# Moving 25 of 35 tile transposes of a gated cross-attention and MLP kernel from TensorE to DRAM and VectorE

## The chip, the cores and the metric

The kernel runs on one core of one Trainium2 chip. The metric is the time of one launch on the device in microseconds (us); lower is better.

## The reference

2048 tokens of 512 features pass through two residual layers, all in float32.

```python
# layer 1: one of 4 experts per token, picked by token id; Wg = Wu = Wd = ctx_2048[e]  (512 x 512)
h = layernorm(x)
z = h @ ctx[e].T
x = x + tanh(g_xattn) * ((silu(z) * z) @ ctx[e].T)
# layer 2: a gated MLP, 512 -> 1408 -> 512
h = layernorm(x)
g = (h @ gate_w.T) * gate_s
u = (h @ up_w.T) * up_s
x = x + tanh(g_ffn) * (((silu(g) * u) @ down_w.T) * down_s)
```

## The kernel before

**Routing.** Up to about 12 us the kernel counts the tokens of each expert and builds index tables. The tokens are laid out so that each tile of 128 belongs to one expert: at most 19 tiles (`STEPS`). `gidx` tells which row of x is in each place, `sidx` where it goes.

**Precision.** A float32 value is split in a high word (ScalarE, a copy to fp32r) and a low word (VectorE, the difference). An expert product has three passes (high by high, low by high, high by low) of four matmuls, `expert_product`, L970. In the MLP the weights have no low words with these inputs, so each product has two passes.

**Expert phase, 12 to 142 us.** In step k TensorE runs `first_product(k)`, the turn of tile k+1's normed rows (`turn_x`, L961, four 128x128 transposes through PSUM, matmuls at L967), `second_product(k-1)`, and `turn_h(k)` (four transposes, L996). VectorE's `step(k)` (L747) is, in order: low word of h of k-1 (L736), norm of k+1 (L684), wait for the gathered rows of k+2, their statistics (L673 and two small ones), `hidden(k)` (L732, wanted by `turn_h(k)`), low word of x of k+1 (L710), and `update(k-1)` (L743), which waits for the second product. ScalarE makes the high words and the silu, and beside them rounds and checks the MLP weights. GpSimd, in a loop of two rounds of six steps (L389), computes 1/std (L362), gathers the rows of tile k+4 (L351) once tile k-2 is stored, and stores tile k-1 (L356) after its update. It copies the two index columns into `inow` at each step (L396, L398). The rows live in a ring of six slots.

**MLP phase, 142 to 389 us.** There are four blocks of four tiles, and each block has 11 chunks of 128 inner features. In chunk c TensorE runs 8 gate and 8 up matmuls (L1077), then the 8 down matmuls of chunk c-1 (L1084). In the first three blocks the tiles of the next block are prepared beside the chunks (`PREP_AT`): statistics and norm at chunks 5 to 8 after the chunk's own VectorE work, `turn_x` on TensorE after the gate and up matmuls of chunks 6 to 9, then high and low words. In block 0 VectorE also makes the low words of the weights (L828). Block 0's own four tiles are turned at the end of the expert phase (L957).

**SyncE's queue** issues plain DMAs in a fixed order, each behind its waits: the expert weights, small inputs, then weight rows (704 KB each) and rows of the down weights to be checked (256 KB each), the rows of the next block, the down weights.

**Counts.** There are 19 + 16 = 35 turns of x, 4 of them by `first_turn_x`, and 19 turns of h.

## Time and profile before

| what | value |
|---|---|
| median of 3 runs | 399.51 us (399.36 to 400.72) |
| the profiled execution | 398.89 us, its span 397.1 us |
| TensorE busy (matmuls, weight loads) | 374.2 us (94%), 305.9 us (77%) |
| VectorE busy | 232.2 us (58%) |
| ScalarE, GpSimd busy | 144.4 us (36%), 84.8 us (21%) |
| mean granted TensorE clock | 0.995 |
| turns of x by L967, 124 matmuls | 19.4 us busy |

Times are of one execution. Busy is the share of the span in which an engine ran an instruction; an engine that has little idle time and ends most waits sets the time.

### The profile page before, as it was taken

What the parts mean: (1) busy time and instruction counts of PE and PEld (TensorE: products, weight loads), DVE (VectorE), ACT (ScalarE), POOL (GpSimd) and SP (SyncE); (2) the same over time, 40 slices, a digit from 0 to 9 for tenths busy, and PEclk for the clock granted to TensorE, in tenths of its full rate; (3) what the DMA queues carried; (4) which work ended last, traced back from release to release, by engine and by line L of the source; (5) the groups of instructions that cost most, each with busy time, mean ns of one, the idle gap of its engine ahead of it and who ended that gap; (6) DMA issues with size and microseconds to landing.
All of it is one profiled execution on the core that took longest, in us unless ns stands there. A gap on an engine that the chain in (4) does not pass through costs nothing.

```text
span 397.1 us, 5787 instructions
## 1 busy us (share of the span) xinstructions
PE 374.2 (94%) x1771; PEld 305.9 (77%) x1771; DVE 232.2 (58%) x441; ACT 144.4 (36%) x263; POOL 84.8 (21%) x130
## 2 busy tenths in 40 slices
PE   3479899999999999999999999999999999999993
PEld 2357688888888878877788888888888888888882
DVE  6878857567877578867647235636225635422225
ACT  4455556565545244522322223322323222222220
POOL 6333544444452120000102101101201001200003
PEclk9999999999999999999999999999999999999998
DMA  6759767461221126210001210000120000100002
GB/s 212 258 188 295 239 210 277 143 213 61 102 79 54 54 83 221 79 68 0 2 1 53 104 55 0 1 0 26 79 106 0 0 0 0 80 26 0 0 0 109
DMA packets 13807, 34.56 MB, mean 87 GB/s; under 512 B 2272, under 2 KB 2272, under 8 KB 13792
## 3 DMA queue, kind: packets, MB, share of 16 engines
q1 hardware_dynamic: 9472, 20.21, 14.9%
q0 software_dynamic: 4320, 14.16, 9.7%
q8 instruction: 8, 0.13, 0.1%
q14 instruction: 7, 0.06, 0.0%
HBM read 25.19 MB, written 9.18 MB: 87 GB/s over the span
## 4 chain that ended last, share of the span: by engine, by line
PE 86%; DVE 6%; DMA 4%; issue 2%; SPq 1%; POOL 1%; ACT 0%; DVEq 0%; POOLq 0%; ACTq 0%
PE bank L1077 39%; PE bank L981 23%; PE bank L1084 19%; PE bank L967 3%; DMA dsb<-down_s 3%; PE bank L996 2%; DVE work L760 1%; DMA rows<-x,gidx 1%; DVE wgu L828 1%; DVE sh L841 1%; PE bank L957 0%; DVE xn L684 0%; DMA ids_i<-ids 0%; DVE rows L875 0%; DVE tmp L868 0%
## 5 line engine op out<-in xcount | busy, mean ns | idle before, releaser
L1077 PE MATMUL bank<-work,wgu 128*128 (+1 forms) x720 | 167.2, 385 | 0.1
L1077 PEld LDWEIGHTS bank<-work,wgu 128*128 128x128 f32 x720 | 133.0, 188 | 27.9 <-issue 0.5
L981 PE MATMUL bank<-work,parts 128*128 (+1 forms) x432 | 111.0, 406 | 2.3 <-DVE work L760 1.5
L981 PEld LDWEIGHTS bank<-work,parts 128*128 128x128 f32 x432 | 79.7, 191 | 19.9 <-issue 2.9
L1084 PE MATMUL bank<-work,hp 128*128 128x512 f32 x352 | 88.5, 394 | 0.5 <-DVE hp L846 0.5
L841 DVE SCALAR_TENSOR_TENSOR sh<-bank,gs,sh 128x512 f32<-128x512 f32 (+1 forms) x45 | 33.2, 738 | 78.8 <-PE bank L1077 78.8
L1084 PEld LDWEIGHTS bank<-work,hp 128*128 128x128 f32 x352 | 65.1, 188 | 13.9 <-DVE hp L846 0.9
L543 ACT ACTIVATE sh<-bank,gs 128x512 f32<-128x512 f32 (+1 forms) x45 | 30.5, 677 | 84.8 <-PE bank L1077 84.0
L547 ACT ACTIVATE hp<-sh 128x512 fp32r<-128x512 f32 (+1 forms) x45 | 28.0, 622 | 88.3 <-DVE sh L841 88.3
L846 DVE TENSOR_TENSOR hp<-sh,hp 128x512 fp32r<-128x512 f32 (+1 forms) x45 | 30.6, 680 | 30.2 <-ACT hp L547 30.0
L362 POOL TENSOR_TENSOR rstd<-ve,half 128x1 f32<-128x1 f32 x31 | 18.6, 599 | 126.7 <-DVE ve L678 126.1
L433 POOL DMA_INDIRECT out<-rows,oidx x16 | 16.1, 1008 | 116.2 <-DVE rows L875 93.6
L743 DVE SCALAR_TENSOR_TENSOR rows<-bank,tg,rows 128x512 f32<-128x512 f32 (+1 forms) x19 | 14.2, 749 | 21.4 <-PE bank L981 21.4
L463 ACT ACTIVATE parts<-bank 128x512 fp32r<-128x512 f32 x19 | 11.4, 599 | 33.0 <-PE bank L996 31.1
L967 PE MATMUL bank<-ident,xn 128*128 128x128 f32 x124 | 19.4, 280 | 3.6 <-DVE xn L684 3.5
L967 PEld LDWEIGHTS bank<-ident,xn 128*128 128x128 f32 x124 | 15.1, 142 | 9.4 <-DVE xn L684 4.8
L684 DVE TENSOR_SCALAR xn<-rows,mv,rstd 128x512 f32<-128x512 f32 (+1 forms) x31 | 16.9, 547 | 9.0 <-POOL rstd L362 9.0
L673 DVE BATCH_NORM_STATS2 bn<-rows 128x6 f32<-128x512 f32 (+1 forms) x31 | 21.2, 685 | 1.5 <-DMA rows<-x,gidx 1.5
L467 ACT ACTIVATE sh<-bank 128x512 f32<-128x512 f32 x19 | 11.4, 598 | 16.6 <-PE bank L981 11.9
L732 DVE TENSOR_TENSOR sh<-bank,sh 128x512 f32<-128x512 f32 x19 | 13.1, 688 | 5.0 <-ACT sh L467 4.6
L356 POOL DMA_INDIRECT x_rows<-rows,inow x12 | 12.3, 1028 | 11.8 <-DVE rows L743 10.0
L351 POOL DMA_INDIRECT rows<-x,inow x12 | 12.5, 1040 | 10.0 <-POOL inow L398 9.2
(126 smaller groups left out, 251.9 us busy)
## 6 DMA issues: line engine op xcount, KB each, us to landing
wraw<-guT SPq DMA_DIRECT2D x8, 704.0 KB
ctx_in<-ctxT SPq DMA_DIRECT2D x4, 1024.0 KB, 5.4
rows<-x_rows SPq DMA_DIRECT2D x8, 512.0 KB, 3.5
checked<-dwT SPq DMA_DIRECT2D x11, 256.0 KB
rows<-dwT SPq DMA_DIRECT2D x11, 256.0 KB, 2.6
dsb<-down_s SPq DMA_DIRECT2D x1, 256.0 KB
out<-rows,oidx POOLq DMA_INDIRECT x16, 2.7
rows<-x,inow POOLq DMA_INDIRECT x12
```

The source lines that it names most:

```text
L362: pool.tensor_tensor(rstd[:, 0:1], ve[:, 0:1], half[:, :], ALU.pow)\
L433: pool.indirect_dma_start(out, bass.IndirectOffsetOnAxis(ap=oidx[:, BLOCK * b + t:BLOCK * b + t + 1], axis=0), rows[:, row_slot(b, t), :], ...
L543: act.activation(sh[:, part], gate_ps(i)[:, part], ACT.Silu, scale=gs[:, 0, c:c + 1])\
L547: act.activation(hslot(c)[:, 0, part], sh[:, part], ACT.Copy)\
L673: dve.bn_stats(bn[:, 0, :], rows[:, ds(at, 1), :]).then_inc(S["bn_parts"], 1)
L684: dve.tensor_scalar(xn[:, :], rows[:, ds(at, 1), :], mv[:, 0, 0:1], rstd[:, 0:1], ALU.subtract, ALU.mult).then_inc(S["xn_ready"], 1)
L841: dve.scalar_tensor_tensor(out=sh[:, part], in0=up_ps(i)[:, part], scalar=gs[:, 1, c:c + 1], in1=sh[:, part], op0=ALU.mult, op1=ALU.mult). ...
L846: dve.tensor_tensor(hslot(c)[:, 1, part], sh[:, part], hslot(c)[:, 0, part].bitcast(F32), ALU.subtract)\
L967: mm = pe.transpose(xt_ps[:, c * P:(c + 1) * P], xn[:, c * P:(c + 1) * P], ident[:, :])
L981: mm = pe.matmul(out_ps[:, :], part(s)[:, c * P:(c + 1) * P], ctx_w(e, c, w), start=n == 0, stop=n == last)
L1077: mm = pe.matmul(out_ps[:, tiles.start * P:tiles.stop * P], wgu[:, row + h, w, c * P:(c + 1) * P], moving, start=n == 0, stop=n == last)
L1084: mm = pe.matmul(acc_ps[u][:, :], hslot(c)[:, s, u * P:(u + 1) * P], down_w(c, w), start=c == 0 and n == 0, stop=c == IC - 1 and n == len( ...
```

## The change

The turns of tiles 6 to 18 and of the 12 tiles of blocks 1 to 3 (25 in all) leave TensorE. The normed rows `xn` (128x512) are written by SyncE to a DRAM scratch in four column quarters (512 runs of 512 B), and read back so that partition 32i+a holds quarter i of rows 4a to 4a+3 (128 runs of 2 KB). One VectorE instruction then transposes all 32x32 blocks. Both sides of it are read and written at a stride of 16 B. In the result, partition p of part c holds feature 4p+c, and so the weights are loaded in that order, and the transposes that stay on TensorE read every fourth column.

VectorE norms a step earlier (k+2) and takes the statistics of k+3 in step k. GpSimd's loop is unrolled, reads the index tables directly, and gathers 16 rows once near its beginning. SyncE's list of loads is interleaved with the write and the read of each tile.

```diff
+TURN_AT = {c + 2: t for c, t in PREP_AT.items()}
+ON_PE = 6
-    ctx_v = ctxT.rearrange("e (c p) f -> e p c f", p=P)
-    gu_v = guT.rearrange("(r p) n -> p r n", p=P)
+    turned = nc.dram_tensor("turned_rows", [TURNED, QUADS, P, P], F32).ap()
+    ctx_v = ctxT.rearrange("e (p c) f -> e p c f", c=KC)
+    gu_v = guT.rearrange("(s p h) n -> s h p n", s=2, h=KC)
+        def every_fourth(a, c):
+            return a[:, :].rearrange("p (q c) -> p c q", c=KC)[:, c, :]
@@ SyncE
-            sp.wait_ge(S["ctx_lo"], EXPERTS * KC)
-            for r in range(5, 2 * KC):
-                check_row(r)
-                weight_row(r)
-            check_row(8)
+            def turn_rows(m):
+                n = m - ON_PE
+                sp.wait_ge(S["xn_ready"], m + 1)
+                sp.dma_start(turned[n].rearrange("i p c -> p i c"),
+                             xn[:, :].rearrange("p (i c) -> p i c", i=QUADS)).then_inc(S["xn_out"], 16)
+                sp.wait_ge(S["xn_out"], 16 * (n + 1))
+                if n:
+                    sp.wait_ge(S["xt_ready"], n)
+                sp.dma_start(quarter_home(m < STEPS),
+                             turned[n].rearrange("i (a g) c -> (i a) (g c)", g=QUADS)).then_inc(S["xq_in"], 16)
-            sp.wait_ge(S["stored"], 16 * (BLOCK + EXPERTS - 1))
-            load_rows(0)
-            for c in range(9, IC):
-                check_row(c)
+            for m in range(ON_PE, STEPS):
+                turn_rows(m)
+                if m - 1 < IC:
+                    check_row(m - 1)
+                if m == 9:
+                    sp.wait_ge(S["ctx_lo"], EXPERTS * KC)
+                if m in (9, 11, 13):
+                    weight_row((m + 1) // 2)
+                if m == 10:
+                    sp.wait_ge(S["stored"], 16 * (BLOCK + EXPERTS - 1))
+                    load_rows(0)
             ...
+                for t in range(BLOCK):
+                    turn_rows(STEPS + BLOCK * (b - 1) + t)
@@ GpSimd
+            pool.memset(inow[:, :], 0).then_inc(S["early_index"], 1)
+            pool.wait_ge(S["early_index"], 1)
+            pool.indirect_dma_start(
+                rows[0:16, ring_slot(5), :], None, x,
+                bass.IndirectOffsetOnAxis(ap=inow[0:16, :], axis=0)).then_inc(S["early_row"], 16)
-            with pool.Fori(0, 2) as i:
-                ...
+            for k in range(2, STEPS + 1):
+                if k < ON_PE:
                     inverse_std(k + 2)
                 if k == NORM_AT:
                     first_inverse_std()
+                pool.wait_ge(S["stored"], 16 * (k - 1))
                 if k + 4 < STEPS:
                     pool.wait_ge(S["x_landed"], 16 * (k + 4 - FIRST))
                     gather(ring_slot(k + 4), gidx[:, k + 4:k + 5])
+                if ON_PE - 1 <= k < STEPS - 3:
+                    inverse_std(k + 3)
                 pool.wait_ge(S["rows_ready"], k)
                 store(ring_slot(k - 1), sidx[:, k - 1:k])
@@ ScalarE
+            def turned_hi(m, home, part):
+                act.wait_ge(S["xt_ready"], m - (ON_PE - 1))
+                act.activation(part, home, ACT.Copy).then_inc(S["xhi_ready"], 1)
@@ VectorE
+            def turn(m, expert):
+                dve.wait_ge(S["xq_in"], 16 * (m - (ON_PE - 1)))
+                dve.wait_ge(S["xlo_ready"], m)
+                dve.transpose(turned_home(expert).rearrange("p (h a g) -> p g h a", h=KC, g=QUADS),
+                              quarter_home(expert).rearrange("p (g b h) -> p g h b", g=QUADS, h=KC))\
+                   .then_inc(S["xt_ready"], 1)
+            def step(k):
+                h_lo(k - 1)
+                norm(k + 2, ring_slot(k + 2))         # waits for xn_out of the tile before
+                landed(k + 3)
+                stats(k + 3, ring_slot(k + 3))
+                turn(k + 1, True)
+                hidden(k)
+                turned_lo(k + 1, True, tile_x(1), tile_x(0))
                 update(k - 1)
             ...
+                    if not last:                      # MLP, ahead of chunk(b, c)
+                        if c in TURN_AT:
+                            next_turn(b + 1, TURN_AT[c])
+                        if c in PREP_AT:
+                            next_stats(b + 1, PREP_AT[c])
+                        if c in TURN_AT:
+                            next_x_lo(b + 1, TURN_AT[c])
+                        if c in PREP_AT:
+                            next_norm(b + 1, PREP_AT[c])
                     chunk(b, c)
@@ TensorE
-                mm = pe.transpose(xt_ps[:, c * P:(c + 1) * P], xn[:, c * P:(c + 1) * P], ident[:, :])
+                mm = pe.transpose(xt_ps[:, c * P:(c + 1) * P], every_fourth(xn, c), ident[:, :])
-                turn_x(k + 1)
+                if turns:
+                    turn_x(k + 1)
-                        if c - 1 in PREP_AT:
-                            with pe.If(b < BLOCKS - 1):
-                                turn_x(STEPS + BLOCK * b + PREP_AT[c - 1])
```

## Rows read from the trace of the kernel before

**Rows 1.** The page: busy shares, and the chain that ended last by engine.
```profile
PE 374.2 (94%) x1771; PEld 305.9 (77%) x1771; DVE 232.2 (58%) x441; ACT 144.4 (36%) x263; POOL 84.8 (21%) x130
PE 86%; DVE 6%; DMA 4%; issue 2%; SPq 1%; POOL 1%; ACT 0%; DVEq 0%; POOLq 0%; ACTq 0%
```

**Rows 2.** Chain in order of time, expert steps: start us, us, what.
```profile
62.66 0.44 PE bank L967 x4
63.10 2.78 PE bank L981 x12
...
69.09 0.44 PE bank L967 x4
```

**Rows 3.** The same chain in block 1 of the MLP.
```profile
229.98 1.81 PE bank L1084 x8
...
235.42 1.81 PE bank L1084 x8
...
240.86 0.44 PE bank L967 x4
241.30 1.85 PE bank L1084 x8
```

**Rows 4.** Timeline of TensorE, block 0: start us, us, engine, line, tiles.
```profile
171.85 1.98 PE L1084 MATMUL bank<-work,hp 128*128 128x512 f32 x8
...
197.03 2.11 PE L1084 MATMUL bank<-work,hp 128*128 128x512 f32 x8
```

**Rows 5.** Timeline of VectorE in an expert step; in brackets idle before.
```profile
59.66 0.75 DVE L743 SCALAR_TENSOR_TENSOR rows<-bank,tg,rows 128x512 f32 x1 [1.47 <-PE bank L981]
...
61.16 0.54 DVE L684 TENSOR_SCALAR xn<-rows,mv,rstd 128x512 f32 x1
...
61.62 0.68 DVE L673 BATCH_NORM_STATS2 bn<-rows 128x6 f32 x1
...
62.66 0.15 DVE L678 TENSOR_SCALAR ve<-mv 128x1 f32<-128x1 f32 x1
...
63.33 0.69 DVE L732 TENSOR_TENSOR sh<-bank,sh 128x512 f32<-128x512 f32 x1 [0.51 <-ACT sh L467]
```

**Rows 6.** GpSimd's DMAs, expert steps: timeline, then landing times of L351, L356.
```profile
61.24 1.00 POOL L356 DMA_INDIRECT x_rows<-rows,inow  x1 [1.08 <-DVE rows L743]
...
65.45 1.03 POOL L351 DMA_INDIRECT rows<-x,inow  x1 [0.83 <-POOL inow L398]
...
77.98 1.04 POOL L351 DMA_INDIRECT rows<-x,inow  x1 [0.85 <-POOL inow L398]
...
83.45 0.18 POOL L396 COPY inow<-gidx 128x1 uint32 x1 [0.70 <-DMA rows<-x,inow]
...
DMA to landing us min/median/max: 3.6/3.9/4.1
...
DMA to landing us min/median/max: 2.7/2.8/4.6
```

**Rows 7.** The page's DMA issues: count, KB each, median us to landing.
```profile
rows<-x_rows SPq DMA_DIRECT2D x8, 512.0 KB, 3.5
...
rows<-dwT SPq DMA_DIRECT2D x11, 256.0 KB, 2.6
```

**Rows 8.** Timeline of VectorE, two chunks of block 0 in a row.
```profile
184.10 0.75 DVE L841 SCALAR_TENSOR_TENSOR sh<-bank,gs,sh 128x512 f32<-128x512 f32 x1 [0.17 <-PE bank L1077]
...
190.29 0.75 DVE L841 SCALAR_TENSOR_TENSOR sh<-bank,gs,sh 128x512 f32<-128x512 f32 x1
```

**Rows 9.** Weight loads of TensorE: a strided f16 operand, a dense f32 one.
```profile
6.55 1.17 PEld L943 LDWEIGHTS bank<-token,is_low 128*128 128x128 f16 x16 [3.08 <-DVE is_low L617]
...
62.27 0.59 PEld L967 LDWEIGHTS bank<-ident,xn 128*128 128x128 f32 x4
```

**Rows 10.** Timeline of the beginning: the second gather, the gates.
```profile
10.58 1.67 POOL L351 DMA_INDIRECT rows<-x,gidx  x1 [0.47 <-DVE gidx L649]
...
26.14 0.20 ACT L506 ACTIVATE tg<-gg 128x2 f32<-128x2 f32 x1 [0.80 <-DMA dsb<-down_s]
```

More of the change, by code:

```diff
@@ L52 @@
 PREP_AT = {5: 0, 6: 1, 7: 2, 8: 3}
+TURN_AT = {c + 2: t for c, t in PREP_AT.items()}
+ON_PE = 6
+TURNED = STEPS - ON_PE + TILES - BLOCK
+QUADS = 4
 def ring_slot(k):
@@ L219, in tile_h, with quarter_home, turned_home @@
             return parts[:, 2 + s, :]
+        def every_fourth(a, c):
+            return a[:, :].rearrange("p (q c) -> p c q", c=KC)[:, c, :]
+        def quarter_home(expert):
+            return xq0[:, :] if expert else rows[:, RING - 2, :]
+        def turned_home(expert):
+            return xt0[:, :] if expert else rows[:, RING - 1, :]
         def ctx_w(e, c, s):
@@ L512, in step @@
                 silu(k)
-                x_hi(k + 1)
-            with act.Fori(1, IC + 1) as k:
+                if on_pe:
+                    x_hi(k + 1)
+                else:
+                    turned_hi(k + 1, turned_home(True), tile_x(0))
+            with act.Fori(1, ON_PE - 1) as k:
+                step(k, on_pe=True)
+                down_check(k - 1)
+            with act.Fori(ON_PE - 1, IC + 1) as k:
                 step(k)
@@ L551, in mlp_block @@
                 for c in range(IC):
+                    if c in TURN_AT and not last:
+                        t = TURN_AT[c]
+                        turned_hi(STEPS + BLOCK * b + t, turned_home(False), xpart(b + 1, (t + 2) % BLOCK, 0))
                     chunk(b, c)
@@ L555, in mlp_block @@
                             down_hi(d)
-                    if c - 1 in PREP_AT and not last:
-                        t = PREP_AT[c - 1]
-                        next_x_hi(STEPS + BLOCK * b + t, b + 1, (t + 2) % BLOCK)
             mlp_block(0, first=True)
@@ L753, in step @@
                 x_lo(k + 1)
+                if k == ON_PE - 2:
+                    norm(k + 2, ring_slot(k + 2))
+                update(k - 1)
+                if k == ON_PE - 2:
+                    landed(k + 3)
+                    stats(k + 3, ring_slot(k + 3))
+            def step(k):
+                looped = not isinstance(k, int)
+                h_lo(k - 1)
+                if looped or k + 2 < STEPS:
+                    norm(k + 2, ring_slot(k + 2))
+                if looped or k + 3 < STEPS:
+                    landed(k + 3)
+                    stats(k + 3, ring_slot(k + 3))
+                turn(k + 1, True)
+                hidden(k)
+                turned_lo(k + 1, True, tile_x(1), tile_x(0))
                 update(k - 1)
@@ L781, in _ @@
             dve.wait_ge(S["gates_ready"], 1)
-            step(1)
+            step_on_pe(1)
             ctx_lo(9, 12)
-            step(2)
+            step_on_pe(2)
             ctx_lo(12, 16)
@@ L787, in _ @@
             dve.tensor_copy(oidx[:, :], bank[4][:, 0:TILES]).then_inc(S["oidx_ready"], 1)
-            with dve.Fori(3, STATS_AT) as k:
+            step_on_pe(3)
+            step_on_pe(4)
+            with dve.Fori(ON_PE - 1, STATS_AT) as k:
                 step(k)
@@ L804, in _ @@
             h_lo(16)
-            norm(18, ring_slot(18))
+            turn(18, True)
             dve.wait_ge(S["loose_step"], 1)
@@ L1034, in _ @@
             for k in range(1, EXPERTS):
-                expert_step(k, *experts_at(k), ctx_ready=KC * (k + 1))
-            with pe.Fori(EXPERTS, 15) as k:
+                expert_step(k, *experts_at(k), ctx_ready=KC * (k + 1), turns=True)
+            expert_step(EXPERTS, *experts_at(EXPERTS), turns=True)
+            with pe.Fori(EXPERTS + 1, 15) as k:
                 expert_step(k, *experts_at(k))
```

93 lines of the change are left out of this document (36 added, 57 removed).

## The prediction

> **What bounds the kernel now.** I read the busy shares first, then the chain that ended last. TensorE is busy 94% of the span and carries 86% of the chain [rows 1]; VectorE, at 58%, has room. So each microsecond taken from TensorE's queue between 28 and 389 us comes back, as long as nothing that feeds TensorE becomes later. I then read the chain in order of time, where the pace is very regular. An expert step is turn 0.44, product 2.78, turn of h 0.44, product 2.78: from the turn at 62.66 to the next at 69.09 are 6.43 us [rows 2]. In the MLP a chunk without a turn takes 5.44 us (229.98 to 235.42), one with a turn in blocks 1 and 2 takes 5.88 (235.42 to 241.30) [rows 3]. In block 0 the timeline shows more: four chunks with turns last from 171.85 to 197.03, 25.18 us, or 6.3 each [rows 4]. There VectorE sets the pace, for its own cycle is 6.19 us, from 184.10 to 190.29, and the turn waits for the norm at its end [rows 8].
>
> **The turns that leave.** Expert phase: 13 turns (tiles 6 to 18) x 0.44 = 5.7 us. Blocks 1 and 2: 8 x (5.88 - 5.44) = 3.5 us. Block 0: 25.18 - 4 x 5.44 = 3.4 us, if VectorE's work there is no longer awaited within the chunk. Gross gain 12.6 us. An expert step would then take 6.43 - 0.44 = 5.99 us.
>
> **The new way of a tile.** Norm, write to DRAM, read back, VectorE transpose. The trace has none of the last three.
> - The write is 256 KB in 512 B runs. Nearest rows: a 256 KB load with 2.6 us [rows 7] and the row stores with 2.7 to 4.6, median 2.8 [rows 6]. I take 2.8.
> - The read is 256 KB in 2 KB runs: 2.6 (512 KB take 3.5 [rows 7], the upper bound).
> - The transpose has 128x512 elements on both sides. By VectorE's passes of that shape it lasts 0.54 to 0.75 [rows 5]; I take 0.69, as a two-input pass, with double (1.4) as the upper end and 0.54 as the lower.
>
> With 0.54 for the norm and 0.1 for each of SyncE's two issues the trip lasts 0.54 + 0.1 + 2.8 + 0.1 + 2.6 = 6.1 us. Norm starts at 61.16 and the statistics after it end at 62.81 [rows 5], so the transpose stands 1.65 us behind the norm's place, one step on: 5.99 + 1.65 = 7.6 us are there. Slack 1.5 us. SyncE is held in its queue during the trip, with a check row, weight row or block rows behind it; each of those is wanted two or more steps later, so I cost this at nothing. The other way round, a weight row of 704 KB or block rows (512 KB, 3.5 us [rows 7]) can lie ahead of the next write, in four steps; the slack covers about 1.5 us of that.
>
> **VectorE in an expert step.** It gains the transpose and loses nothing. Before, it stood idle 1.47 ahead of the update and 0.51 ahead of `hidden` [rows 5], together 1.98 of 6.43; now 5.99 - (6.43 - 1.98) - 0.69 = 0.85 idle is left. It still fits, but `hidden(k)`, which `turn_h(k)` waits for, now stands behind the transpose and behind the wait for the gathered rows of tile k+3, one tile further ahead than before. This is the tightest place of the change. The chain, from the end of a second product: update 0.21 + 0.75 (the product ended at 62.66 - 2.78 - 0.44 = 59.44, the update at 59.66 + 0.75 = 60.41 [rows 2, 5]), store's issue 0.83 later at 61.24, landing 2.8, gather's start 0.83, landing 3.6, statistics 1.19 (61.62 to 62.81), transpose 0.69, hidden 0.69: 11.6 us [rows 5, 6]. Two steps are 12.0. So the slack is 0.4 us. Before, the chain had a whole step more. Not every gather lands in 3.6: the one at 77.98 was waited for until 83.45, 5.5 us, as block rows were loading [rows 6], and DRAM traffic now grows by 512 KB per step. Some gathers will be late by about 1 us. There are 11 such steps; I take a quarter late by 0.9: 2.5 us lost. The ends are 0 and 11 x 0.8 = 8.5 (next part).
>
> **The crossing.** Tile 6 is the first to take the trip. Its norm stands behind the low word of x in step 4. In step 6 that ends near 64.6 (0.6 behind `hidden`, 63.33 + 0.69), two steps of 6.43 earlier at 51.7. So the transpose can start at 51.7 + 6.1 = 57.8 and `hidden(5)` ends at 59.2. `turn_h(6)` started at 65.88 (63.10 + 2.78); `turn_h(5)`, a step and a turn earlier, wants its input at 59.0 [rows 2, 5]. With the handovers 0.5 us is lost once (0 to 2.5, with a 4.6 us write).
>
> **Strided reads.** 19 turns of h and 10 of x stay on TensorE and now load every fourth f32, a stride of 16 B. The nearest row: 16 loads of 128 f16 columns at a stride of 32 B last 1.17 us, 73 ns each [rows 9], below the 110 ns (0.44/4) at which dense transposes follow each other [rows 2]. So I expect nearly nothing: 29 x 0.035 = 1.0 us. The upper end is a doubled turn, 29 x 0.44 = 12.8. A gain has no source here: lower end 0.
> On this stride the Trainium skill speaks against the change: "Advanced Engine Details and Errata", SBUF Cachelines, has 16-byte lines of which each needs two hits in a row for full rate, and here each gets one. The strided row at 73 ns leaves that open, since its elements are half as wide. If the rule holds fully for the f32 loads, it is the second rival below.
>
> **Block 0's VectorE.** The transpose adds 0.69 to 6.19, but the low word of x now stands between statistics and norm and fills the wait for GpSimd's 1/std; I take 6.4 us for chunks 7 and 8, 5.7 for 5 and 6, 5.2 for 9. Against 5.44 it falls behind by at most 2.5 us. TensorE first notices when the product behind down 1.81 and gate 1.81 waits for `h`, 0.75 long: 3.62 - 0.75 = 2.9 us. So it is hidden; 0.3 for the near miss, 1.5 if the transpose takes 1.4.
>
> **Beginning.** The extra gather can shorten the second one's issue (1.67 against the usual 1.03 [rows 6, 10]), but 1/std of tile 0 waits for statistics anyway: 0, at the ends -0.7 and +0.7. The copies to `inow` that go free GpSimd 0.36 us per step; counted in the chain above. Expert weights in 8 KB runs may land earlier and with them the scales that ScalarE waited 0.80 for [rows 10]: gain 0.3 (0 to 0.8).
>
> **The sum.** 12.6 - 2.5 - 0.5 - 1.0 - 0.3 + 0.3 = 8.6. The profiled execution took 398.89, so 390.3; the median of the runs is 0.6 above it: **390.9 us**.
>
> **Rivals.**
> 1. *The gather chain sets every step.* If landings are 5.5 us throughout, the chain is 13.5, a step 6.75 in 11 steps: 11 x (6.75 - 5.99) = 8.4 lost in place of 2.5: 396.8. For it: the slack of 0.4 and more traffic. Against: most landings at 3.6 to 4.1 [rows 6], and fewer loads after step 12.
> 2. *Strided f32 reads run at half rate.* 12.8 in place of 1.0: 402.7, slower than before. Against it: the 73 ns.
> 3. *The trip is too long* (the other side as well). It decides from 6.43 + 1.65 = 8.1 us on: then `hidden` waits in each expert step for the read. With a write of 4.6 [rows 6] and a read of 3.5 [rows 7] plus 0.7 for the norm and issues, 8.8, a step is 7.15, 13 x (7.15 - 5.99) = 15.1 lost in place of 2.5 for gathers: 403.5. MLP chunks have two chunks, 10.9 us, for the trip, so no loss there. Against it: both medians.
>
> **Chances.** Forecast 0.66, first rival 0.15, second 0.08, third 0.08, something else 0.03. About 0.5% (2.0 us) can be told from no change, so faster means below 397.5: 0.66 and most of the first rival, 0.76. Same 0.11, slower 0.13. The lower end of the range is the gain without losses, 12.6 + 0.8 = 13.4: 386. The upper, 400, takes in the first rival and a mild form of the others.
>
> **What would show it.** Right: expert steps of 6.0 us in the chain, with no wait of TensorE's transposes of h for `hidden`; L967's count down from 124 to 24 matmuls; chunks of 5.44 in all blocks. Wrong: the transpose far over 0.7; TensorE waiting for `hidden`, and VectorE ahead of it for gathered rows (first rival) or for the read (third); transposes of more than 0.44 per four (second). The prediction falls if an expert step is above 6.3 us, or the transpose above 1.4.

## The result, and the profile after

The changed kernel takes 403.67 us (401.01 to 406.84, 11 runs) where the kernel before takes 399.30 (398.06 to 400.72, 11 runs): ratio 1.0112, 95% interval 1.0077 to 1.0147. 390.9 was predicted, the range ended at 400. It is slower by 1.1%, though TensorE has 100 fewer matmuls to do. The medians and ratios below leave out executions that took over 1.5% more than the fastest of the same kernel (one of `before_traffic`, two of `copy_turn`, one of `all_dense_late`).

The profiled execution took 403.7 us, its span is 402.0 (before 397.1), its mean granted clock 0.984 (before 0.995). The page of the changed kernel, busy shares and chain by engine, answers to [rows 1]:

```profile
PE 370.5 (92%) x1671; PEld 301.8 (75%) x1671; DVE 257.8 (64%) x466; ACT 146.4 (36%) x263; POOL 84.0 (21%) x108
PE 63%; DVE 15%; DMA 13%; issue 4%; ACT 2%; POOL 2%; DVEq 0%; SPq 0%; POOLq 0%
```

TensorE's busy time fell by only 3.7 us for 100 matmuls less, and its share of the chain from 86% to 63%. DMAs now hold 13%. The chain says where: it runs through stores and gathers of the expert phase (7% and 3%).

**Where the time went.** Three marks in both traces divide the span: the turn of h of tile 4 (52.86 before, 52.39 after), the first gate matmul of the MLP (142.53 and 152.04) and the end (397.1 and 402.0). The beginning gained 0.5 us. The expert steps between the first two marks went from 89.67 to 99.65 us: 10.0 lost. The MLP went from 254.6 to 250.0: 4.6 gained. The sum is the 4.9 us of the spans. So one half of the change does nearly what it should, and the other loses more than that.

Timeline of TensorE in the changed kernel's expert phase (start us, us, engine, line, tiles; in brackets the idle time before and what ended it). It answers to [rows 2]. L1064 is the turn of h, L1049 the products:

```profile
60.09 0.75 PE L1064 MATMUL bank<-ident,sh 128*128 128x128 f32 x4 [1.57 <-DVE sh L773]
61.01 7.37 PE L1049 MATMUL bank<-work,parts 128*128 x24 [0.17 <-issue]
...
90.22 0.74 PE L1064 MATMUL bank<-ident,sh 128*128 128x128 f32 x4 [3.43 <-DVE sh L773]
91.10 7.34 PE L1049 MATMUL bank<-work,parts 128*128 x24
99.38 0.75 PE L1064 MATMUL bank<-ident,sh 128*128 128x128 f32 x4 [0.94 <-DVE sh L773]
100.30 5.70 PE L1049 MATMUL bank<-work,parts 128*128 x24 [0.17 <-issue]
...
107.87 0.75 PE L1064 MATMUL bank<-ident,sh 128*128 128x128 f32 x4 [1.87 <-DVE sh L773]
108.75 7.38 PE L1049 MATMUL bank<-work,parts 128*128 x24
...
122.62 5.73 PE L1049 MATMUL bank<-work,parts 128*128 x24
...
128.57 5.75 PE L1049 MATMUL bank<-work,parts 128*128 x24
```

The last two rows are a step of the size that was predicted: 128.57 - 122.62 = 5.95 us. Earlier TensorE waits for `hidden` (L773), four times between 60 and 108: 1.57, 3.43, 0.94 and 1.87, together 7.8 us. And behind each of the three longer waits the next 24 matmuls last 7.4 us in place of 5.7: another 4.9 us. The turn of h behind a wait is slower too: 0.9 us from its start to the product's (60.09 to 61.01) in place of 0.39 (128.18 to 128.57); once, at 80.17, it is so without a wait. Windows of the same trace show what the slow products are (busy us of PE, PEld, DVE, ACT, POOL, then the granted clock, the DMA share, GB/s):

```profile
75.00:100.00 25.00, 20.32 (x84) 15.73 (x82) 15.31 (x27) 11.62 (x24) 6.31 (x8) 0.93 0.79 246
...
125.00:150.00 25.00, 25.00 (x126) 20.93 (x125) 21.64 (x40) 12.35 (x23) 6.86 (x8) 1.00 0.40 127
```

Windows of 1 us show it plainly: the granted clock is 1.00 up to 61 us, 0.62 from 61 to 62, 0.50 from 62 to 64, 0.67 from 64 to 65 and 1.00 from 65 on; behind the other two long waits it is 0.50 from 92 to 95, and 0.51 and 0.50 from 109 to 112. So after these idle times the engine was granted its lower level (1.2 of 2.4 GHz) for some 3 us of the next product. The expert steps of before have no such wait and no such product. The wait's price is thus not its length: 1.57 us of waiting cost 1.57 + 0.5 for the turn + 1.6 for the product.

The eight steps from 52.78 to 116.36 take 63.6 us, 15.8 more than eight of 5.97; less the 5.7 that 13 turns gained, that is the 10.0 lost. Of the 15.8, 7.8 are waits, 4.9 slow products and 2.6 slow turns (five of 0.5).

**What `hidden` waits for.** GpSimd's timeline: L391 stores, L386 gathers, L397 is 1/std.

```profile
82.66 0.96 POOL L386 DMA_INDIRECT rows<-x,gidx  x1 [6.02 <-DMA x_rows<-rows,sidx]
83.65 0.58 POOL L397 TENSOR_TENSOR rstd<-ve,half 128x1 f32<-128x1 f32 x1
84.41 1.05 POOL L391 DMA_INDIRECT x_rows<-rows,sidx  x1 [0.18 <-issue]
91.93 0.97 POOL L386 DMA_INDIRECT rows<-x,gidx  x1 [6.47 <-DMA x_rows<-rows,sidx]
...
93.68 1.04 POOL L391 DMA_INDIRECT x_rows<-rows,sidx  x1 [0.18 <-issue]
```

From store to store are 93.68 - 84.41 = 9.3 us, and ahead of the stores GpSimd waits for nothing (0.18, "issue"): it isn't VectorE's updates that are late but GpSimd's own loop, and of its 9.3 us 7.3 are the landing of the store, without which the next gather may not start (the gather overwrites the slot). The other parts of the loop (gather's issue, 1/std, handovers) take 2.0. The chain that ended last passes through this loop three times before it comes back to `hidden`:

```profile
75.60 6.81 DMA x_rows<-rows,sidx
...
82.66 0.96 POOL rows L386
...
84.41 7.26 DMA x_rows<-rows,sidx
...
93.68 7.72 DMA x_rows<-rows,sidx
...
101.66 3.31 DMA rows<-x,gidx
...
106.13 1.13 DVE xt L756
...
107.27 0.56 DVE sh L773
```

Landing times of the stores (L391) in the changed kernel, to be read beside the last of [rows 6]:

```profile
DMA to landing us min/median/max: 2.7/3.4/7.7
```

The medians of the stores (2.8 and 3.4) hide it; the long ones, 6.8, 7.3 and 7.7 us, follow each other. (The 4.6 of [rows 6] is the very first store, at 36.1 us; from 60 to 130 us the stores of before take 2.7 to 3.4.) The gathers are less late: those issued at 82.66 and 91.93 are there when VectorE's statistics, which wait for them, start at 87.35 and 96.48, so 4.7 and 4.6 us. The landing row of the gathers in [rows 6] (3.6/3.9/4.1) holds only the two at 9.0 and 10.6 us, ahead of the expert steps. The first of TensorE's four waits, at 60.09, is another: its chain goes through the write of the first trip, 3.87 us from 51.74, and then norm, statistics and transpose. SyncE's queue shows what goes beside them (L316 read of the trip, L292 check row, L323 block rows, L285 weight row, L311 write of the trip):

```profile
83.16 0.33 SPq L316 DMA_DIRECT2D xq<-turned_rows  x1
83.57 0.38 SPq L292 DMA_DIRECT2D checked<-dwT  x1
84.01 0.95 SPq L323 DMA_DIRECT2D rows<-x_rows  x2
85.11 0.55 SPq L311 DMA_DIRECT2D turned_rows<-xn  x1
92.44 0.33 SPq L316 DMA_DIRECT2D xq<-turned_rows  x1
92.87 0.38 SPq L292 DMA_DIRECT2D checked<-dwT  x1
93.30 0.43 SPq L285 DMA_DIRECT2D wraw<-guT  x1
94.17 0.38 SPq L311 DMA_DIRECT2D turned_rows<-xn  x1
```

SyncE is held by the trip: from 85.11 to 92.44 it waits for the write of the trip to land (7.3 us, where 2.8 was assumed; an undisturbed one at 119.0 took 2.2), and then four to five transfers go out within 2 us, at 84 and at 93, just as GpSimd issues its store. From 75 to 100 us the DMA engines are busy for 0.79 of the time, from 125 to 150 for 0.40. That the trips' bytes make the stores late is so far a reading of one trace; experiment 3 tests it.

**VectorE's transposes**, groups of the changed kernel (xcount | busy us, mean ns | idle before):

```profile
L756 DVE STREAM_TRANSPOSE xt<-xq 128x512 f32<-128x512 f32 x13 | 14.7, 1128 | 1.0 <-DMA xq<-turned_rows 0.9
L756 DVE STREAM_TRANSPOSE rows<-rows 128x512 f32<-128x512 f32 x12 | 13.3, 1105 | 0.0
```

1.13 and 1.11 us, not 0.69. **The MLP**: the chain in block 1 answers to [rows 3], and VectorE's in block 0 to [rows 8]:

Block 1, start us, us, what:

```profile
229.67 3.63 PE bank L1146 x16
233.30 1.81 PE bank L1153 x8
235.11 3.63 PE bank L1146 x16
```

Block 0:

```profile
187.69 0.76 DVE sh L902
...
194.55 0.76 DVE sh L902
...
201.41 0.76 DVE sh L902
```

Chunks of 5.44 in blocks 1 and 2, as predicted; but 6.86 us for VectorE's cycle in chunks 7 and 8 of block 0, where 6.4 was expected and 6.19 was before.

### The profile page after: what moved, and what is told of

It is laid out like the page before. It is cut to its first block, busy times and chain, and to the rows that moved or that the text cites. A ratio compares the mean times of both kernels' runs of the same rounds, so it can differ in the third digit from the quotient of the medians.

```text
span 402.0 us, 5526 instructions
## 1 busy us (share of the span) xinstructions
PE 370.5 (92%) x1671; PEld 301.8 (75%) x1671; DVE 257.8 (64%) x466; ACT 146.4 (36%) x263; POOL 84.0 (21%) x108
## 4 chain that ended last, share of the span: by engine, by line
PE 63%; DVE 15%; DMA 13%; issue 4%; ACT 2%; POOL 2%; DVEq 0%; SPq 0%; POOLq 0%
PE bank L1146 31%; PE bank L1153 15%; PE bank L1049 15%; DMA x_rows<-rows,sidx 7%; DMA rows<-x,gidx 3%; DVE wgu L889 2%; DMA rows<-dwT 2%; DVE work L819 1%; DVE sh L902 1%; PE bank L1064 1%; DVE bn L705 1%; POOL rstd L397 1%; ACT hp L579 1%; DMA turned_rows<-xn 1%; DVE xt L756 1%
## 5 line engine op out<-in xcount | busy, mean ns | idle before, releaser
L1049 PE MATMUL bank<-work,parts 128*128 (+1 forms) x432 | 111.6, 414 | 2.9 <-DVE work L819 1.4
L1049 PEld LDWEIGHTS bank<-work,parts 128*128 128x128 f32 x432 | 84.1, 199 | 22.7 <-issue 4.2
L1153 PE MATMUL bank<-work,hp 128*128 128x512 f32 x352 | 87.1, 389 | 0.5 <-DVE hp L907 0.5
L397 POOL TENSOR_TENSOR rstd<-ve,half 128x1 f32<-128x1 f32 x31 | 21.1, 679 | 104.8 <-DVE ve L710 102.5
L386 POOL DMA_INDIRECT rows<-x,gidx x19 | 20.0, 1051 | 46.8 <-DMA x_rows<-rows,sidx 38.7
L391 POOL DMA_INDIRECT x_rows<-rows,sidx x19 | 19.4, 1022 | 35.9 <-DVE rows L784 28.7
L1064 PE MATMUL bank<-ident,sh 128*128 128x128 f32 x72 | 12.2, 292 | 9.5 <-DVE sh L773 9.5
L1064 PEld LDWEIGHTS bank<-ident,sh 128*128 128x128 f32 x72 | 10.8, 207 | 12.4 <-DVE sh L773 11.6
L480 ACT ACTIVATE work<-rows 128x512 f32 (+1 forms) x12 | 7.6, 632 | 27.1 <-DVE rows L756 27.1
```

The lines of the kernel that those rows point to most:

```text
L386: pool.indirect_dma_start(rows[:, at, :], None, x, bass.IndirectOffsetOnAxis(ap=index, axis=0))\
L391: pool.indirect_dma_start(scratch, bass.IndirectOffsetOnAxis(ap=index, axis=0), rows[:, at, :], None)\
L397: pool.tensor_tensor(rstd[:, 0:1], ve[:, 0:1], half[:, :], ALU.pow)\
L1049: mm = pe.matmul(out_ps[:, :], part(s)[:, c * P:(c + 1) * P], ctx_w(e, c, w), start=n == 0, stop=n == last)
L1064: mm = pe.transpose(ht_ps[:, c * P:(c + 1) * P], every_fourth(sh, c), ident[:, :])
L1153: mm = pe.matmul(acc_ps[u][:, :], hslot(c)[:, s, u * P:(u + 1) * P], down_w(c, w), start=c == 0 and n == 0, stop=c == IC - 1 and n == len( ...
```

## The experiments

All were timed beside the kernel before, whose median is given with each (398.8 to 399.3). Theory stands for the explanation of the moment; it changed on the way.

**1. The two halves apart.** `mlp_only` is the kernel before with the 12 MLP turns moved and the new feature order; experts and GpSimd as before.

```diff
+ON_PE = STEPS                       # tiles 0 to 18 stay on TensorE
```


> Only the 12 turns of the MLP phase go by DRAM and VectorE; the expert phase, GpSimd's loop and SyncE's early order are those of the kernel before (the strided reads of the turns left on TensorE stay). Theory (the loss of the whole change lies in the expert phase, +10.0 us there, and the MLP phase gained 4.6): about 4 us faster than before, near 395.5, with chunks of 5.44 us in blocks 1 and 2. Rival (the DRAM trips or the longer VectorE queue cost in the MLP phase too, or the strided reads cost): no gain, 398 to 401.

Measured 395.94 against 398.92, ratio 0.9909 (0.9877 to 0.9941), as the theory had it. So the MLP half gains 3.0 us net, and the expert half loses 403.7 - 395.9 = 7.8 by itself.

**2. Traffic, and late statistics.** `small_trip` is the changed kernel, with the trips cut to 8 columns of a row; `stats_late` puts the wait for the gathered rows behind `hidden`.

```diff
 # small_trip
-  sp.dma_start(turned[n].rearrange(...), xn[:, :]...)
+  sp.dma_start(turned[n, 0][:, 0:8], xn[:, 0:8])
 # stats_late: step(k)
-  landed(k + 3); stats(k + 3, ...)
   turn(k + 1, True)
   hidden(k)
+  landed(k + 3); stats(k + 3, ...)
```


> The kernel after, with every write and read of the trip cut to 8 columns (4 KB in place of 256 KB) and the transpose reading a constant tile, so the output is not the reference's. All waits, the order of the queues and the 1.13 us transposes stay. Theory (the 512 KB per step, in one burst with a weight row, a check row and GpSimd's store, hold the store up to 7.7 us and so set GpSimd's loop at 9.3 us): stores land in about 3 us again, the expert phase from turn_h(4) to the first gate matmul falls from 99.7 to about 88 us, total 391 to 393. Rival (the longer VectorE chain or the later weight rows make the steps long, not the traffic): at most 3 us gained, total over 399.

> The kernel after, with the wait for gathered rows and the statistics of tile k+3 moved behind hidden(k). Theory (GpSimd's own loop of store, landing, gather, 1/std sets the period in steps 8 to 11): steps there stay near 9 us, the total moves by less than 2 us from 403.7. Rival (hidden(k) standing behind the gather wait sets the steps): the wait of turn_h for hidden, 9.5 us, goes, total 394 to 397.

Measured 398.88 against 398.92 (0.9985, 0.9954 to 1.0016): the bytes of the trips are worth 4.8 us. The theory had 391 to 393 and missed by 6: without the trips' bytes the three stores from 77 to 93 us still land in 4.5, 6.1 and 6.3 us, beside the held loads. `stats_late`: 399.66 (1.0006, 0.9975 to 1.0036): 4.0 us, where the theory gave under 2. It had taken GpSimd's loop for the sole bound; but a part of its lateness is passed on only since `hidden` stands behind the wait for rows that it doesn't need. And with that wait gone another shows. VectorE waited 0.9 us in all for the reads of the trips in the changed kernel, in `stats_late`:

```profile
DVE xt L756 <- DMA xq<-turned_rows: 8.6, 7, 2.7
```

(us in total, times, longest.) Its longest chain to `hidden` is a trip: a write of 7.65 us from 86.07 and a read of 4.19 behind it. The trip's own lateness stood hidden behind the store's.

**3. The same traffic in the kernel before.** `before_traffic` makes all of the expert trips (nothing uses them) with SyncE's order of the changed kernel; the turns stay on TensorE. `before_hold` is the same with trips of 8 columns.

```diff
+  for m in range(6, STEPS):
+      trip(m)                       # write xn, wait, read back; 8 columns in before_hold
+      if m - 1 < IC: check_row(m - 1)
+      ...                           # weight rows at 9, 11, 13, block rows at 10
```


> The kernel before, with the trip's write and read of 256 KB each added for tiles 6 to 18 at the places of the kernel after in SyncE's queue, their data unused. Norm waits for the write of the tile before. TensorE still turns, and statistics keep their old place. Theory (traffic alone holds up GpSimd's stores, but the old order has a step more of slack in front of the statistics): stores land in 5 us or more in steps 8 to 11, yet GpSimd's loop then sets a few of the steps too, so 3 to 8 us slower than before, 402 to 407. Rival (the loss comes from the new order of VectorE, which the old order does not have): within 1.5 us of before although the stores land late.

> The kernel before with SyncE's queue held as in the kernel after (same waits, same order of check, weight and block rows behind the trip of each tile 6 to 18), but the trip is 8 columns (4 KB) each way. The same with full 256 KB trips took 410.0 us, 11 us over before. Theory (both are needed: the held queue puts the large loads next to GpSimd's store, and the 512 KB lengthen the burst): 1 to 4 us over before, stores landing in up to 6 us. Rival (holding alone does it): 8 us or more over before. Other rival (traffic alone): within 0.5 us of before.

Measured 409.51 against 398.92 (1.0218, 1.0159 to 1.0278), above the theory's 402 to 407, and 400.38 against 398.78 (1.0049, 1.0024 to 1.0073). The profiled executions are the longest of `before_traffic` (412.05) and the shortest of `before_hold` (398.47); so their traces show the kind of the difference, the medians its size. Landing times of the stores in `before_traffic`:

```profile
DMA to landing us min/median/max: 2.7/4.5/8.8
```

and in `before_hold`:

```profile
DMA to landing us min/median/max: 2.7/2.8/3.7
```

This is the clearest pair: the same waits, the same order of loads, and 9.1 us between them by the medians (6.7 by the ratios, from three executions). GpSimd's store to store time with traffic, in steps whose own work is unchanged (L372 stores):

```profile
78.32 1.00 POOL L372 DMA_INDIRECT x_rows<-rows,inow  x1 [0.30 <-issue]
...
88.52 1.01 POOL L372 DMA_INDIRECT x_rows<-rows,inow  x1 [0.30 <-issue]
...
99.86 1.00 POOL L372 DMA_INDIRECT x_rows<-rows,inow  x1 [0.31 <-issue]
```

10.2 and 11.3 us where a step is 6.43. So the traffic makes a loss of this kind without VectorE's new order and without the unrolled loop, and the chain of this trace runs through the stores' landings; what the new order adds is the 4.0 us of `stats_late`. The held queue alone costs 1.6 (1.0 to 2.9 by the interval). Whether the changed kernel would lose less with GpSimd's old loop wasn't tried.

**4. Spreading the burst.** `weights_early` issues the last three weight rows in steps 6, 7 and 8 (from 9, 11, 13); `two_quarters` gives the trip two landing buffers, so that SyncE's read doesn't wait for the transpose before; `two_quarters_late` adds the late statistics.

```diff
 # weights_early
-  if m in (9, 11, 13): weight_row((m + 1) // 2)
+  if m in (6, 7, 8):   weight_row(m - 1)
 # two_quarters
-  if n: sp.wait_ge(S["xt_ready"], n)
+  free = n - 1 if m < STEPS else n
+  if free > 0: sp.wait_ge(S["xt_ready"], free)
```


> The kernel after, with weight rows 5, 6 and 7 issued behind tiles 6, 7 and 8 in place of 9, 11 and 13. Theory (bursts that hold a weight row or block rows beside the trip hold up the stores): the late stores move to the steps near 56 to 75 us and the steps after 100 us become 6 to 6.5 us; the total moves by -3 to +1 us. Rival (the trip's own traffic is enough, whatever lies beside it): the stores stay at 7 us in steps 9 to 11, total unchanged within 1 us.

> The kernel after with two buffers for the read quarters in the expert phase, so that SyncE issues the read as soon as the write has landed and no longer waits for the transpose of the tile before; the check, weight and block rows behind it are issued up to 3 us earlier, away from GpSimd's store. VectorE's steps 5 to 9 are unrolled for it. Theory (the large loads collide with the store by the held queue): 2 to 5 us faster than after, 399 to 402. Rival (the number of bytes per step decides, not the moment): within 1 us of after.

> two_quarters, and the statistics of tile k+3 behind hidden(k) as in stats_late, which gave 4 us alone. Theory (the two remedies act on different waits): 395 to 397, as good as the kernel that moves only the MLP's turns. Rival (both remove the same stalls): no better than stats_late, 399 to 401.

Measured: `weights_early` 407.24 against 399.17 (1.0182), 3.6 us worse than the changed kernel, a miss: TensorE waits 10.6 us for `hidden` in its trace, in place of 7.8. That 704 KB more beside a trip cost more than they saved later is the likely reading, not a tested one. `two_quarters` 401.80 against 398.78 (1.0074, 1.0046 to 1.0101), `two_quarters_late` 398.94 (0.9985, 0.9964 to 1.0006), not the 395 to 397 of its theory and no better than `stats_late` by more than the noise. Its stores still take up to 7.3 us to land, but the chain that ended last hardly goes through them any more: from 50 to 145 us it holds 19.6% of writes and 11.7% of reads of the trip and 4.9% of stores, where the changed kernel has 4.1% of writes and 22.9% of stores. Its longest wait for `hidden`, 4.0 us at 95.88, stands behind a write of 7.6 and a read of 4.5 us. With late statistics it is the trip itself that is too long.

**5. The smaller terms.** `copy_turn` puts a dense elementwise pass in the transpose's place. `pool_only` and `stride_only` are the kernel before with GpSimd's part, and with the new feature order and strided reads of TensorE, alone.

```diff
 # copy_turn
-  dve.transpose(turned_home(expert)..., quarter_home(expert)...)
+  dve.tensor_tensor(turned_home(expert), quarter_home(expert), quarter_home(expert), ALU.max)
 # stride_only
-  xn[:, c * P:(c + 1) * P]
+  every_fourth(xn, c)
```


> The kernel after, with the 32x32 transpose replaced by a dense elementwise pass of the same tile (about 0.68 us in place of 1.13), so the output is not the reference's. Theory (GpSimd's loop sets the disturbed steps, VectorE only the chunks of block 0): 1 to 3 us faster than after, 401 to 402.5. Rival (the transpose, 0.44 us over the 0.69 that was reckoned, sets the steps): 13 x 0.44 and more, 6 us or more faster.

> The kernel before with GpSimd's part alone changed: loop unrolled, index tables read directly, one gather of 16 rows near the beginning. Theory (GpSimd is not on the path in the kernel before): within 1 us of before, the beginning up to 0.5 us earlier. Rival (the early gather makes the first gathers cheaper, or the unrolled code costs): 1.5 us or more to either side.

> The kernel before with the new feature order alone: weights and expert weights loaded in that order, all 54 turns on TensorE reading every fourth column. Four transposes went from 0.44 to 0.48 us in the trace of after. Theory: 54 x 0.04 = 2 us slower, 401 to 402, if the extra shows in every turn. Rival (the skill's rule of 16-byte lines holds in full, a turn doubles): 54 x 0.44 = 24 us slower. Other rival: no difference, as the expert weights land earlier in 8 KB runs.

Measured: `copy_turn` 400.75 against 399.17 (1.0047, 1.0013 to 1.0081): the 0.44 us that each transpose takes beyond the assumed 0.69 is worth 2.9 us (2.6 by the ratios). In the traces the first gate matmul comes 1.5 us earlier (150.50 for 152.04) and the MLP takes 1.6 less. `pool_only` 398.67 (0.9994, 0.9981 to 1.0008): nothing. `stride_only` 400.43 (1.0040, 1.0025 to 1.0056): 1.3 us for 54 turns. Its group of TensorE's weight loads, to be read beside the 0.59 us for four of [rows 9]:

```profile
L971 PEld LDWEIGHTS bank<-ident,xn 128*128 128x128 f32 x124 | 19.4, 206 | 7.6 <-DVE xn L688 4.1 <-issue 1.7
```

A strided load takes 206 ns, a dense one 0.59 / 4 = 148 in that row and 142 on average in the same group of the kernel before, but the turn only goes from 0.44 to 0.47 us.

**6. Why the transpose is slow.** `dense_transpose` is `mlp_only` with dense operands of the transpose. The other two keep the reference's feature order: in `mlp_dense_in` the norm writes its columns in quarter order, so that the transpose reads densely; `mlp_dense` also reads the rows back in another order, in four DMAs with runs of 512 B, so that it writes densely too. TensorE reads without a stride in both.

```diff
 # dense_transpose
-  dve.transpose(turned_home().rearrange("p (h a g) -> p g h a", ...), quarter_home().rearrange("p (g b h) -> p g h b", ...))
+  dve.transpose(turned_home(), quarter_home())
 # mlp_dense_in: norm, then the input of the transpose
+  to = to.rearrange("p (i c b) -> p c i b", i=QUADS, c=KC)
+  frm = frm.rearrange("p o (c i b) -> p (o c) i b", i=QUADS, c=KC)
-  quarter_home().rearrange("p (g b h) -> p g h b", ...)
+  quarter_home().rearrange("p (g h b) -> p g h b", ...)
 # mlp_dense: further
+  for i in range(QUADS):
+      sp.dma_start(quarter_home()[32 * i:32 * i + 32, :].rearrange("a (g c) -> a g c", g=QUADS),
+                   turned[n][:, P * i:P * i + P].rearrange("(g a) c -> a g c", g=QUADS))
-  turned_home().rearrange("p (h a g) -> p g h a", ...)
+  turned_home().rearrange("p (h g a) -> p g h a", ...)
```


> mlp_only (396 us) with VectorE's transpose reading and writing dense columns in place of every fourth, so the blocks are laid out wrongly. Theory (the 1.10 us of the transpose are the operation's own): the transpose stays at 1.0 to 1.15 us, the total within 0.5 us. Rival (the 16 B stride on both sides slows it, by the skill's rule of 16-byte lines): 0.6 to 0.7 us, and 1 to 2 us less in total, out of block 0.

> Before's feature order and dense TensorE reads everywhere, the 12 MLP turns moved as in the change; the norm writes its columns in the order quarter, chunk, 32 (runs of 128 B), so that the transpose reads dense rows; it still writes with a stride of 16 B. Theory (each side's stride costs the same): transposes of 0.9 us. Rival 1 (the read's stride costs all 0.40): 0.70. Rival 2 (the write's): 1.10. The strided reads of TensorE that go are worth 1.4 us, so 394 to 395 by either, 395.9 less 1.4 = 394.5.

> As the one before it, and the read of the trip takes rows in another order (four DMAs with runs of 512 B; the write has runs of 2 KB), so that the transpose is dense on both sides. Theory: transpose 0.70 us; chunks 5 to 9 of block 0, where VectorE sets the pace, become 0.40 shorter each, so 1 to 1.6 us beside the 1.4 of the strided reads: 395.9 - 1.4 - 1.3 = 393.2. Rival (runs of 512 B on the read make the trip longer than the two chunks it has): TensorE waits in the chunks, 395 to 397.

Measured: `dense_transpose` 394.31 against 398.78 (0.9871, 0.9842 to 0.9900), its transposes 0.70 us, both as the rival had it; `mlp_dense_in` 394.34 against 399.25 (0.9869, 0.9844 to 0.9894); `mlp_dense` 392.82 against 399.25 (0.9842, 0.9819 to 0.9864). The group of the transposes in `mlp_only`:

```profile
L760 DVE STREAM_TRANSPOSE rows<-rows 128x512 f32<-128x512 f32 x12 | 13.3, 1107 | 0.0
```

in `mlp_dense_in`:

```profile
L760 DVE STREAM_TRANSPOSE rows<-rows 128x512 f32<-128x512 f32 x12 | 12.9, 1079 | 0.0
```

and in `mlp_dense`:

```profile
L761 DVE STREAM_TRANSPOSE rows<-rows 128x512 f32<-128x512 f32 x12 | 8.5, 704 | 0.0
```

The stride of 16 B costs 0.03 us on the read (1.11 to 1.08) and 0.38 on the write: the second rival of `mlp_dense_in`. `mlp_dense` gains 6.4 us on the kernel before, and is the fastest that computes the whole.

**7. What is left of the loss.** `small_late` takes both causes away: trips of 8 columns, two buffers, late statistics. `from_13` is the changed kernel, with the trips of the expert phase begun at tile 13, behind the weight and block rows.

```diff
 # from_13
-ON_PE = 6
+ON_PE = 13
```


> The changed kernel with double quarter buffers, statistics of tile k+3 behind the hidden product, and trips of 8 columns (it leaves out the rest of the trip; the transposes read another buffer): neither the traffic nor the wait of hidden for gathered rows is left. Theory: small trips alone gave 398.9, late statistics alone 399.7, against 403.7; the two causes overlap, since late rows hurt through that wait, so together 395 to 397. Rival (they are independent and add up): 403.7 - 4.8 - 4.0 = 394.9 or less, down to the 390.9 predicted.

> The changed kernel with ON_PE = 13 in place of 6: tiles 6 to 12 keep their turn on TensorE and SyncE's loads go in the order of before; only tiles 13 to 18 and the 12 MLP tiles take the trip. Theory (the loss comes from trips beside weight rows, check rows and block rows, in steps 5 to 11): the remaining trips meet only the stores and gathers, so the time is that of the version with the MLP turns alone (395.9) less 6 x 0.44 = 2.6, plus up to 2 for the crossing: 393.5 to 395.5, with expert steps of 6.43 up to the crossing and 6.0 behind it. Rival (a gather that leads by one step less, with the crossing, costs it wherever it stands): the crossing alone takes 2 + 1.9 for the clock and stores land at over 5 us again: 397 to 400.

`small_late` took 390.94 against 399.25 (0.9799, 0.9777 to 0.9821), 12.7 less than the changed kernel. The theory of overlapping causes (395 to 397) was wrong; so was a plain addition (394.9), as the two together give more than their sum. That it meets the 390.9 of the prediction to the tenth is chance: it has slower transposes than were predicted, and fewer waits. Its timeline of TensorE has steps of 5.98 us (65.83 to 71.81) in the same part:

```profile
65.83 5.75 PE L1051 MATMUL bank<-work,parts 128*128 x24
71.42 0.63 PE L1066 MATMUL bank<-ident,sh 128*128 128x128 f32 x4
71.81 5.75 PE L1051 MATMUL bank<-work,parts 128*128 x24
```

So the trips' bytes, that wait and the single buffer are all that stands between the changed kernel and the pace that was predicted. Of 12.7 us, late statistics with a second buffer give 4.8 (403.7 to the 398.9 of `two_quarters_late`), and the bytes behind them the other 8.0; without late statistics the bytes gave 4.8 (`small_trip`), so neither cause shows its full price while the other is there. Cutting the bytes does two things at once: it takes traffic from beside the stores, and it makes the trip itself short. By the traces the second is most of the 8.0, for the stores of `small_late` still land in up to 6.3 us, and its TensorE waits 0.2 us in all for `hidden`. No run separates the two. `from_13` took 395.12 (0.9912, 0.9888 to 0.9936), within its theory. It has one wait of 1.46 us for `hidden` in the expert phase, at the crossing, with no slow product behind it. Against the 395.94 of `mlp_only` it isn't told apart: six turns fewer on TensorE bring 0.8 by the medians and nothing by the ratios (0.9912 and 0.9909).

**8. Put together.** `from_13_dense` joins what helped; `all_dense_late` makes all 25 trips in the dense form, with two buffers and late statistics.

```diff
 # both: the edits of mlp_dense, for the expert tiles too; in step(k):
-  landed(k + 3); stats(k + 3, ...)
   turn(k + 1, True)
   hidden(k)
+  landed(k + 3); stats(k + 3, ...)
 # from_13_dense: ON_PE = 13; all_dense_late: ON_PE = 6 and two buffers
```


> from_13 with everything that helped alone: before's feature order, the norm of a travelling tile in quarter order, the trip read in four DMAs, so that the transpose is dense (0.70) and TensorE reads without a stride; the statistics of tile k+3 behind the hidden product. Theory (gains add up): the version with the MLP turns alone and dense is at 392.8, and starting the expert's trips at tile 13 gained 0.8 more with strides; with 0.4 us shorter transposes and late statistics nothing of the 6 x 0.44 = 2.6 is lost again: 390 to 391.5. Rival (the crossing's cost, a wait of 1.5 us and the clock behind it, stays): 392 to 393.

> All 25 trips as in the changed kernel, with double quarter buffers, late statistics and the dense form (all transposes 0.70, no strided reads on TensorE). Theory (late stores and gathers by the traffic stay in steps 5 to 11, and only the stride's cost goes): 398.9 - 1.4 (TensorE's reads) - 1.3 (block 0) = 396, still above the 392.8 of the MLP turns alone. Rival (shorter transposes and the write's longer runs, 2 KB in place of 512 B, shorten the bursts enough): 391 to 394.

Measured 393.29 against 399.31 (0.9833, 0.9797 to 0.9868) for `from_13_dense`, near its rival: no better than `mlp_dense`. And 403.27 (1.0087, 1.0057 to 1.0117) for `all_dense_late`, 7 us above its theory and 9 above its rival. Waits of VectorE from 50 to 155 us in `two_quarters_late` (us in total, times, longest):

```profile
DVE xt L760 <- DMA xq<-turned_rows: 8.3, 9, 3.0
```

and in `all_dense_late`:

```profile
DVE xt L765 <- DMA xq<-turned_rows: 22.9, 10, 3.1
```

The read in four DMAs with runs of 512 B arrives later than the one with runs of 2 KB, 2.3 us per wait in place of 0.9, and beside the expert phase's loads that eats more than the dense transpose brings. The trace shows where it goes: SyncE needs 1.75 us to issue the four (83.59 to 85.34), where one takes 0.33, and those 1.4 us are the difference of the waits. In the chain from 50 to 145 us these issues hold 13.2%, writes 38.6% and reads 16.6%. A single DMA with runs of 512 B wasn't tried, so what the runs do beside it is open. In the MLP, with two chunks of cover, the same read is never waited for.

## Why the prediction was wrong, step by step

- **The turns that leave.** The gross gain of 12.6 holds where it can be seen: undisturbed expert steps are 5.95 to 5.98 (5.99 predicted), chunks 5.44. The prediction's own sign of being wrong, an expert step above 6.3 us, came true: steps of 8.2, 7.6, 6.0, 6.5, 10.0, 9.2, 8.45 and 7.6 in the first eight.
- **VectorE in an expert step: the step that failed.** It was named as "the tightest place", and its loss sized at 2.5 us with an end of 8.5. Two things were wrong in it. The sum used 2.8 us for the store's landing and let only gathers be late, and at most 5.5; but "DRAM traffic now grows by 512 KB per step" bears on the store as well, which took 6.8, 7.3 and 7.7 us in a row. The store's landing holds GpSimd, and GpSimd's own loop was never summed: landing + 2.0, so that it sets the step once a store takes over 5.99 - 2.0 = 4.0 us, and at 7.3 it takes the 9.3 that were seen. (The 3.6 us for a gather was read from the two at the beginning; in the burst it was 4.7.) And the price of a wait was taken for its length, where the three long ones cost 1.6 more each by the clock and 0.5 by the slower turn. Runs that show it: `before_traffic` against `before_hold` for the bytes and the stores, `stats_late` for the place of `hidden`, `small_late` for both.
- **SyncE "held in its queue ... I cost this at nothing".** Nearly right as to the queue (`before_hold`: 1.6 us). What it does beside the traffic is read from the trace: it lets the held loads go in a burst with the trip.
- **The trip.** 6.1 us were given; undisturbed writes take 2.2 (2.8 assumed) and reads 2.6 as assumed (medians of `mlp_only`), in the burst a write takes 7.3. The third rival has this mechanism with a write of 4.6, and its 403.5 is the time that was measured; but that is luck, for VectorE hardly waited for the read (0.9 us in all, of 13 transposes), as the late rows stood ahead of it. Only with late statistics does the trip set the pace (8.6 us of waits in `stats_late`). The first rival names the right place, the chain of store and gather, but has the gather late and not the store, with 396.8 as its price. The second rival's 402.7 is near as well, and `stride_only` excludes it.
- **The crossing.** 0.5 us, 2.5 at most: the wait was 1.57, the slower turn and product behind it 2.1, so 3.7. In `from_13` it was a wait of 1.46 with no slow product.
- **Transposes.** 0.69 assumed with an upper end of 1.4; 1.11 to 1.13 measured, since the write has a stride. Worth 2.6 to 2.9 us (`copy_turn`), half of it in the expert phase by the traces; the sum had no term for it.
- **Strided reads of TensorE.** 1.0 predicted for 29 turns; 1.3 measured for 54. Right in kind. The rule of the Trainium skill ("Advanced Engine Details and Errata", SBUF Cachelines) that accesses which each go to another 16-byte line pay a penalty is borne out by the loads (142 to 206 ns), but most of that lies beside the matmuls. For VectorE the traces agree with it only for the write; the read at the same stride (1.08 against 1.11) shows no penalty.
- **Block 0.** 3.1 us were to be gained (3.4 - 0.3). Its transposes of 1.1 us and GpSimd's 1/std of 0.93 keep VectorE at 6.86 in two chunks; all that TensorE's chunks of block 0 last beyond 5.44 each is 2.8 us in the trace after and 3.6 before, a gain of 0.7. With dense transposes and reads the MLP half brings 6.4 in all (`mlp_dense`), where the terms of the prediction were 3.5 + 3.4 - 0.3 = 6.6.
- **Beginning.** +0.3 predicted, +0.5 in the trace; GpSimd's part alone (`pool_only`) shows no difference.

By size, of the 12.8 us between forecast and result: the spans put 2 on the MLP (4.6 gained where 6.6 were expected) and the rest on the expert steps. That the rest is the trips' bytes and the wait for late rows is shown by `small_late`; how it divides between store, trip and clock is read from single traces (7.8 us of waits, 4.9 of slow products and 2.6 of slow turns in the changed kernel) and not separated by a run.

## What to carry to other kernels

Work moved off the bound engine by way of DRAM must be costed against every DMA that the critical loop awaits, the short ones first: take the row of their longest landing, not of the median, and look for the instruction that can't go on until it lands. Sum the loop of each engine that issues such DMAs, and ask at which landing time it becomes longer than a step (here 4.0 us, while the longest store of before took 4.6); and see which transfers a landing row really holds. Once one wait is taken away, look for the next: here the trip stood behind the store. Start such trips where the loads are over and where they have a stage or two of cover (here the MLP), and keep a wait for far-ahead data behind the work that is wanted now. Price a wait of TensorE with the slow turn and product behind it, too: here 2.1 us on top of waits of 1.6 to 3.4. Count the issues of a transfer that is cut in parts: here 1.4 us for three more.

## What the runs showed of the hardware that was not expected

- VectorE's transpose of 128x512 f32 takes 0.70 us with a dense write and 1.08 to 1.13 with a write at a stride of 16 B, whatever the read's stride.
- After idle times of 1.57, 1.87 and 3.43 us TensorE's next 24 matmuls took 7.4 us in place of 5.7 (granted clock 0.50 for some 3 us, as from 62 to 64); after one of 0.94, and after one of 1.46 in `from_13`, they took 5.7.
- A store of 128 rows of 2 KB that lands in 2.8 us (median) in the kernel before takes up to 7.7 in the changed kernel, beside trips and block or weight rows (DMA share 0.79 from 75 to 100 us), and up to 8.8 in `before_traffic`.
- Reading 256 KB in four DMAs with runs of 512 B made VectorE wait 22.9 us in all where one DMA with runs of 2 KB made it wait 8.3. SyncE takes 1.75 us to issue four and 0.33 for one.
